# The second mixture-of-experts layer computed in units of 640 slots instead of tiles of 128

## The reference

```python
cap = int(1.25 * N / E)                       # 640
probs = softmax(x @ gate_w.T)
top2_w, top2_idx = top_k(probs, 2)
counts = bincount(a_e, length=E)
keep = counts <= cap                          # an expert with more tokens than that gives nothing
buf = zeros((E, cap + 1, H)).at[a_e, p].set(x[tok_id])
h = silu(einsum('ech,efh->ecf', buf, w1) + b1[:, None, :])
y = einsum('ecf,egf->ecg', h, w2) + b2[:, None, :]
contrib = y[a_e, p] * (a_w * valid)[:, None]
out = contrib.reshape(N, 2, H).sum(axis=1)
```

## Time and profile before

| | us |
|---|---|
| median of three runs | 2154.68 |
| the profiled execution | 2156.69 |
| its span, first to last instruction | 2154.9 |
| first gather of the second experts starts | 1972.19 |
| last scatter of the second experts starts | 2112.67 |
| the sums are read back, first DMA issued | 2119.80 |
| PE, DVE, ACT, POOL busy over the whole span | 1854.9, 1239.3, 914.2, 438.1 |

### The profile page before, as it was taken

One profiled execution on the slowest core, in us unless ns is written; L12 is line 12 of the kernel. 1 busy time (PEld: TensorE's weight loads), 2 busy tenths in 40 slices (PEclk: granted clock), 3 DMA queues, 4 the chain that ended last, 5 costly groups with the idle time before them and its releaser, 6 DMA issues. The chain is left out here.

```text
span 2154.9 us, 35159 instructions
## 1 busy us (share of the span) xinstructions
PE 1854.9 (86%) x9600; PEld 1119.4 (52%) x9601; DVE 1239.3 (58%) x2822; ACT 914.2 (42%) x1337; POOL 438.1 (20%) x573
## 2 busy tenths in 40 slices
PE   7899999999999999996599999999994885068771
PEld 4423333333333333363388888888884565037550
DVE  4588888888888888744711111111113796946335
ACT  3336666666666667753022233223331520031330
POOL 2210000000000000030023333333331001202771
PEclk9979999999999999998799999999997998586995
DMA  4511111111111111054433433443442001141224
GB/s 148 182 45 31 30 37 30 30 36 31 30 34 33 30 33 33 16 164 142 159 90 110 111 99 104 115 114 108 97 111 80 1 1 63 63 153 27 46 38 156
DMA packets 103317, 159.34 MB, mean 74 GB/s; under 512 B 20704, under 2 KB 79392, under 8 KB 97760
## 3 DMA queue, kind: packets, MB, share of 16 engines
q1 hardware_dynamic: 69712, 118.46, 16.9%
q0 software_dynamic: 22656, 24.51, 6.5%
q10 hardware_dynamic: 10896, 15.73, 2.1%
HBM read 124.19 MB, written 49.02 MB: 80 GB/s over the span
## 5 line engine op out<-in xcount | busy, mean ns | idle before, releaser
L552 DVE TENSOR_REDUCE unit_max<-ps_ring 128x1 f32<-128x512 f32 x1024 | 655.4, 686 | 83.7 <-PE ps_ring L429 73.4
L538 ACT ACTIVATE w<-ps_scores 128x1024 f32<-128x1024 f32 x512 | 510.0, 1023 | 266.2 <-PE ps_scores L504 254.4
L429 PE MATMUL ps_ring<-k_stack,q_stack 96*128 96x512 bf16 x1024 | 371.7, 391 | 9.8 <-POOL v_padded L392 9.2
L504 PE MATMUL ps_scores<-q_stack,k_stack 98*128 98x512 bf16 x1024 | 305.7, 380 | 0.1
L1495 PE MATMUL m_ps_h<-m_xt,m_w 128*128 128x256 f32 x1248 | 278.0, 381 | 0.8 <-DVE m_xt L1546 0.8
L1507 PE MATMUL m_ps_y<-w,m_ht 128*128 x1248 | 275.8, 379 | 0.0
L451 PE MATMUL ps_o<-w,v_padded 128*32 128x512 f32 x2048 | 272.8, 605 | 0.6 <-ACT w L538 0.6
L429 PEld LDWEIGHTS ps_ring<-k_stack,q_stack 96*128 96x128 bf16 x1024 | 102.1, 100 | 317.3 <-DVE unit_max L552 232.2
L1495 PEld LDWEIGHTS m_ps_h<-m_xt,m_w 128*128 128x128 f32 x1248 | 238.6, 191 | 34.0 <-DVE m_xt L1546 1.2
L1507 PEld LDWEIGHTS m_ps_y<-w,m_ht 128*128 128x128 f32 x1248 | 234.2, 190 | 30.3
L1527 ACT ACTIVATE m_ht<-m_ps_h,m_w 128x256 f32<-128x256 f32 x312 | 131.0, 471 | 143.7 <-PE m_ps_h L1495 143.7
(11 more groups left out here) (230 smaller groups left out, 2008.9 us busy)
## 6 DMA issues: line engine op xcount, KB each, us to landing
m_w<-in_w SPq DMA_DIRECT2D x39, 1028.0 KB
rows<-g_rows SPq DMA_DIRECT2D x16, 512.0 KB, 2.9
y<-sums SPq DMA_DIRECT2D x16, 512.0 KB, 7.1
q_parts<-qk_part SPq DMA_DIRECT2D x16, 384.0 KB, 3.6
k_parts<-qk_part SPq DMA_DIRECT2D x16, 384.0 KB, 3.8
q_stack<-q_parts SPq DMA_DIRECT2D x64, 96.0 KB
k_stack<-k_parts SPq DMA_DIRECT2D x64, 96.0 KB
xt<-in_xt ACTq DMA_DIRECT2D x8, 512.0 KB, 4.2
```

Source lines behind the costliest of these rows:

```text
L429: nc.tensor.matmul(out[:, :], qs[0:STACK, u, qt * P:(qt + 1) * P], ks[0:STACK, u, half * HALF:(half + 1) * HALF], start=True, stop=True).t ...
L504: mm = nc.tensor.matmul(p_s[kt % 2][:, half * HALF:(half + 1) * HALF], ks[:, u, kt * P:(kt + 1) * P], qs[:, u, half * HALF:(half + 1) * HALF],
L538: nc.scalar.activation(pt[:, kt, :], p_s[kt % 2][:, :], ACT.Exp, scale=SCALE)\
L552: nc.vector.tensor_reduce(unit_max[:, u % 2, half, qt:qt + 1], src[:, :], axis=AX.X, op=ALU.max).then_inc(ring_used, 1)
```

## The change

The stage is written anew as `stage_experts_columns`. Its unit is an expert: 640 slots.

- The five gathers of an expert are issued together, those of expert e+1 before the scatters of expert e, and each has an index tile of its own. They signal per PSUM bank: chunks 0 and 1, chunks 2 and 3, chunk 4.
- The weights stand and the tokens stream, 320 at a time (two halves of an expert). The first product thus has its features on the partitions, and the turn back and its copy are gone. The bias is a per-partition operand of ScalarE's SiLU, which reads PSUM itself; VectorE's bias addition is gone. The bias is loaded as 128 x 16 values and no longer as 128 x 2048.
- VectorE copies the turned tokens out of PSUM instead of ScalarE, 512 columns at a time.
- The second product is unchanged per 128 tokens, but has two PSUM tiles in turn. `m_y` holds a whole expert, twice.
- The five scatters of an expert follow each other without a wait between them. Before the first one GpSimd waits for those of the expert before.
- `indices(e)` copies ten index columns for an expert at once. It waits until all scatters of expert e-2 have landed, and it stands on VectorE behind the second biases of expert e-2.
- The stage is written out for all 8 experts, without a loop, and without the separate semaphore instructions.

```diff
-def stage_experts(nc, c, tiles, fixed, F, w1, w2, b1, b2, func, rows, sums):
...
+def stage_experts_columns(nc, c, per, w1, w2, b1, b2, func, rows, sums, finish=None):
+    FC, T = D // P, per * P
+    TH = T // 2
+    BANKS = (per + 1) // 2
+    with ExitStack() as stack:
+        mem = Mem(nc, stack)
+        ig = [mem.sb(f"m_ig{j}", [P, 1], I32) for j in range(2 * per)]
+        isc = [mem.sb(f"m_is{j}", [P, 1], I32) for j in range(2 * per)]
+        xg = [mem.sb(f"m_x{u}", [P, per, D]) for u in range(2)]
+        xt = [mem.sb(f"m_xt{u}", [P, KC, T]) for u in range(2)]
+        ht = [mem.sb(f"m_ht{u}", [P, FC, T]) for u in range(2)]
+        ys = [mem.sb(f"m_y{u}", [P, per, D]) for u in range(2)]
+        p_x = [mem.ps(f"m_ps_x{n}") for n in range(BANKS)]
+        p_h = [mem.ps(f"m_ps_h{f}") for f in range(FC)]
+        p_y = [mem.ps(f"m_ps_y{n}") for n in range(2)]
+        idx_g, idx_s = mem.sem("m_idx_g"), mem.sem("m_idx_s")
+        gathered = [[mem.sem(f"m_gathered{u}{n}") for n in range(BANKS)] for u in range(2)]
+        added = mem.sem("m_added")
+        x_turned, x_copied = mem.sem("m_x_turned"), mem.sem("m_x_copied")
+        h_made, act_done = mem.sem("m_h_made"), mem.sem("m_act_done")
+        y_made, y_biased, y_scaled = mem.sem("m_y_made"), mem.sem("m_y_biased"), mem.sem("m_y_scaled")
+        def chunks(n):
+            return range(2 * n, min(2 * n + 2, per))
+        def bank_of(half):
+            return (0, 1) if half == 0 else (2,)
+        with nc.Block() as block:
+            @block.gpsimd
+            def _(pool):
+                def gather(e):
+                    for j in range(per):
+                        pool.wait_ge(idx_g, e * per + j + 1)
+                        pool.indirect_dma_start(out=xg[e % 2][:, j, :], out_offset=None, in_=rows,
+                                                in_offset=bass.IndirectOffsetOnAxis(ap=ig[e % 2 * per + j][:, :], axis=0))\
+                            .then_inc(gathered[e % 2][j // 2], 16)
+                def add(e):
+                    wait_from(pool, added, e * per * 16)
+                    for j in range(per):
+                        pool.wait_ge(idx_s, e * per + j + 1)
+                        pool.wait_ge(y_scaled, e * per + j + 1)
+                        pool.indirect_dma_start(out=sums,
+                                                out_offset=bass.IndirectOffsetOnAxis(ap=isc[e % 2 * per + j][:, :], axis=0),
+                                                in_=ys[e % 2][:, j, :], in_offset=None, bounds_check=N - 1,
+                                                oob_is_err=False, compute_op=ALU.add).then_inc(added, 16)
+                gather(0)
+                for e in range(E):
+                    if e + 1 < E:
+                        gather(e + 1)
+                    add(e)
+                if finish is None:
+                    pool.wait_ge(added, E * per * 16)
 ...
+            @block.tensor
+            def _(pe):
+                def turn_x(e, n):
+                    pe.wait_ge(gathered[e % 2][n], (e // 2 + 1) * len(chunks(n)) * 16)
+                    wait_from(pe, x_copied, (e - 1) * BANKS + n + 1)
+                    for k in range(KC):
+                        for j in chunks(n):
+                            at = (k * 2 + j % 2) * P
+                            mm = nc.tensor.transpose(p_x[n][:, at:at + P], xg[e % 2][:, j, k * P:(k + 1) * P],
+                                                     c.ident[:, :])
+                    mm.then_inc(x_turned, 1)
+                def first_product(e, half):
+                    pe.wait_ge(x_copied, e * BANKS + bank_of(half)[-1] + 1)
+                    for f in range(FC):
+                        wait_from(pe, act_done, (2 * e + half - 1) * FC + f + 1)
+                        for k in range(KC):
+                            mm = nc.tensor.matmul(p_h[f][:, 0:TH], w1[:, e * KC + k, f * P:(f + 1) * P],
+                                                  xt[e % 2][:, k, half * TH:(half + 1) * TH],
+                                                  start=(k == 0), stop=(k == KC - 1))
+                        mm.then_inc(h_made, 1)
+                def second_product(e, j):
+                    pe.wait_ge(act_done, (2 * e + ((j + 1) * P > TH)) * FC + FC)
+                    wait_from(pe, y_biased, e * per + j - 1)
+                    for f in range(FC):
+                        mm = nc.tensor.matmul(p_y[(e * per + j) % 2][:, 0:D], ht[e % 2][:, f, j * P:(j + 1) * P],
+                                              w2[:, e * FC + f, :], start=(f == 0), stop=(f == FC - 1))
+                    mm.then_inc(y_made, 1)
+                for n in range(BANKS):
+                    turn_x(0, n)
+                for e in range(E):
+                    first_product(e, 0)
+                    first_product(e, 1)
+                    for j in range(per):
+                        second_product(e, j)
+                        if j >= per - BANKS and e + 1 < E:
+                            turn_x(e + 1, j - (per - BANKS))
+            @block.scalar
+            def _(act):
+                def middle(e, half):
+                    for f in range(FC):
+                        act.wait_ge(h_made, (2 * e + half) * FC + f + 1)
+                        nc.scalar.activation(ht[e % 2][:, f, half * TH:(half + 1) * TH], p_h[f][:, 0:TH], func,
+                                             bias=b1[:, e * FC + f:e * FC + f + 1]).then_inc(act_done, 1)
+                def scale(e, j):
+                    t = e * per + j
+                    act.wait_ge(y_biased, t + 1)
+                    nc.scalar.activation(ys[e % 2][:, j, :], ys[e % 2][:, j, :], ACT.Copy,
+                                         scale=c.gains[:, t:t + 1]).then_inc(y_scaled, 1)
+                for e in range(E):
+                    middle(e, 0)
+                    middle(e, 1)
+                    for j in range(per):
+                        scale(e, j)
 ...
+            @block.vector
+            def _(dve):
+                def indices(e):
+                    wait_from(dve, added, (e - 1) * per * 16)
+                    for j in range(per):
+                        nc.vector.tensor_copy(ig[e % 2 * per + j][:, :], c.gather[:, e * per + j:e * per + j + 1])\
+                            .then_inc(idx_g, 1)
+                    for j in range(per):
+                        nc.vector.tensor_copy(isc[e % 2 * per + j][:, :], c.scatter[:, e * per + j:e * per + j + 1])\
+                            .then_inc(idx_s, 1)
+                def copy_x(e, n):
+                    dve.wait_ge(x_turned, e * BANKS + n + 1)
+                    cols = len(chunks(n)) * P
+                    nc.vector.tensor_copy(xt[e % 2][:, :, n * 2 * P:n * 2 * P + cols],
+                                          p_x[n][:, :].rearrange("p (c n) -> p c n", c=KC)[:, :, 0:cols])\
+                        .then_inc(x_copied, 1)
+                def bias_y(e, j):
+                    t = e * per + j
+                    dve.wait_ge(y_made, t + 1)
+                    nc.vector.tensor_tensor(ys[e % 2][:, j, :], p_y[t % 2][:, 0:D], b2[:, e, :], ALU.add)\
+                        .then_inc(y_biased, 1)
+                indices(0)
+                indices(1)
+                for n in range(BANKS):
+                    copy_x(0, n)
+                for e in range(E):
+                    for j in range(per):
+                        bias_y(e, j)
+                        if j >= per - BANKS and e + 1 < E:
+                            copy_x(e + 1, j - (per - BANKS))
+                    if e + 2 < E:
+                        indices(e + 2)
+        mem.clear()
...
-            b1 = m.sb("b1_1", [P, E, D])
+            b1 = m.sb("b1_1", [P, E * KC])
...
-                act.dma_start(b1[:, :, :], a.b1_1.partition_broadcast(P)).then_inc(loaded, 16)
+                act.dma_start(b1[:, :], a.b1_1).then_inc(loaded, 16)
...
-            stage_experts(nc, c, CAP * E, CAP, D, w1, w2, b1, b2, ACT.Silu, rows[1], sums[1])
+            stage_experts_columns(nc, c, CAP, w1, w2, b1, b2, ACT.Silu, rows[1], sums[1])
```

More of the change, by code:

```diff
@@ L1166, in stage_experts @@
         y_made, y_biased, y_scaled = mem.sem("m_y_made"), mem.sem("m_y_biased"), mem.sem("m_y_scaled")
-        spare_p = mem.sem("m_spare")
-        halves = F // HW
+        def chunks(n):
+            return range(2 * n, min(2 * n + 2, per))
+        def bank_of(half):
+            return (0, 1) if half == 0 else (2,)
         with nc.Block() as block:
-            def steps(eng, body):
-                peeled_ends(eng, tiles // STEP, body)
             @block.gpsimd
             def _(pool):
[L1176 to L1205, removed]
-                        elif u - 1 in (0, fixed):
-                            wait_apart(pool, spare_p, added[0], before[0])
-                            wait_apart(pool, spare_p, added[1], before[1])
-                        add(t + u - 1, (u - 1) % 2)
-                steps(pool, body)
```

(39 more changed lines are left out.)

117 lines of the change are left out of this document (7 added, 110 removed).

## The result

The kernel after takes 2159.44 us, median of 17 runs (2155.43 to 2167.17), against 2154.96 for the kernel before (2152.97 to 2158.85, 17 runs): ratio 1.0023, 95% interval [1.0013, 1.0032]. A second set gave 1.0024 [1.0012, 1.0036]. The forecast was 2158.3 with 2149 to 2166 and "the same", up to 2159.0, as the likeliest. By the two intervals the change costs 3 to 8 us; whether that is more than the 0.2% that the prediction drew as its line isn't decided.

A forecast was written before the change was run, and what follows sets the result against it. GpSimd's preparation of 80 transfers was taken as the bound. The stage: 17.3 + 12.45 + 89.0 + 13.9 + 3.9 + 7.5 = 144.05 us against 140.48; thus 2154.68 + 3.6 = 2158.3 us, range 2149 to 2166.

The forecast's parts named there:

- the 3.6 us that the stage was to lose: Second experts' stage, first gather to last scatter's start: 144.05 us forecast against 140.48 before.
- GpSimd's preparation is the bound, and stays: Second experts: GpSimd's serial preparation of 40 gathers and 40 scatters sets the pace before and after; chance 0.74.
- The 0.30 us stays: GpSimd's gap before each transfer remains without separate semaphore instructions; rival: the gathers' gap goes, 12 us faster, chance 0.12.
- The beginning, 17.3 us: Stage's start: first scatter 17.3 us after the first gather, between 16.4 (full clock) and 18.4 (half clock until 1985.4).
- The border: Between experts GpSimd waits 2.9 us for the landing and 1.0 to the gather: cycle 17.8 us instead of 16.66.
- the rival of the shorter border: Between experts GpSimd answers in 0.5 us: 3.5 us less, 2155; its chance is included in the 0.74.
- The last border, 3.9 us: From expert 6's fifth scatter to expert 7's first: 3.9 us, waiting for the landing.
- The stage, +3.6 us: Second experts, first gather to last scatter's start: 144.05 us against 140.48, 3.6 us more.
- The landings: Rival at seven borders: five scatters in flight land slower, 3.95 us for an empty one; 7 us more, 2165; chance 0.05.
- What stands behind is the same.: Everything after the stage's last scatter takes the same time, so only the stage's 3.6 us is added.
- TensorE at half clock: Rival in the expert cycles: TensorE at half clock becomes the bound, 20.8 us against 17.8; 2169 to 2179; chance 0.07.
- The rule on descriptors: Rival: descriptor generation is small, scatters overlap, TensorE sets the pace at full clock; 50 us less, 2105; chance 0.02.

The follow-up runs named there:

- 80 more turns: The kernel before with the ten transposes of each expert's middle layer done twice: 2155.27 us, ratio 1.0001.
- 448 unused bytes: The kernel after with 448 unused bytes per partition behind the second experts' biases, so the store's tiles start at a multiple of 512: 2157.47 us, ratio 1.0005.
- indices early: The kernel after with gather index copies ahead of the second biases, without a wait: 2149.36 us; with own scatter index tiles too: 2148.97 us.
- TensorE kept busy: The kernel after with 15 extra fp32 products per expert (1 to 6) into an unread PSUM bank: 2157.55 us, ratio 1.0011 to before.
- gathers two ahead: The kernel with all indices early, plus a third gather buffer and an index tile per gather, gathers running two experts ahead: 2148.81 us, ratio 0.9966 to before.
- the gathers-two-ahead one with the tiles moved: The kernel with gathers two experts ahead, plus 448 unused bytes that put the store's tiles at a multiple of 512: 2144.89 us, ratio 0.9949 to before.

## Why the prediction was right

The time lies in the range, and the mechanism in the stage is the one forecast: GpSimd runs dry at each border, because the gather indices wait for the scatters. That the number came so close (2158.3 against 2159.4) is luck: of the 3.6 us that the stage was to lose, the profiles show 0.7 on average, and the rest of the 4.5 us lies where nothing was forecast.

- *GpSimd's preparation is the bound, and stays.* Right: 101.4 us for 80 instructions, cycles free of other idle once the wait is gone, 80 more turns at no cost.
- *The 0.30 us stays.* Right: it stands between instructions with no wait of their own (0.30 <-issue). That rival fell.
- *The beginning, 17.3 us.* 16.7, 18.2 and 18.4 in the three profiles of after (the third with 448 unused bytes); the bounds were 16.4 and 18.4. The 16 records of the first products took 5.29, 6.73 and 6.75 us, at a granted clock up to the first scatter of 0.69, 0.63 and 0.63.
- *The border.* Forecast 2.9 to the landing and 1.0 to the answer, cycle 17.8; measured 17.08. Three profiles have 1.62 us of idle there where 2.3 were forecast. The mis-sized term is the answer: the gather starts 0.43 us after the copy (2005.11 to 2005.54, 2040.88 to 2041.31); the landing took 2.74. The 1.0 had been read from the stage's first gather, where it is 0.72 in after as well (1976.42 to 1977.14), and from a scatter behind ScalarE, and neither is a gather at a border. Five cycles: 85.4 us instead of 89.0. This is the rival of the shorter border, an answer in 0.5 us for 3.5 us less and 2155: it came true. At the first border, behind expert 0, 4.95 were forecast from the last scatter's start to the gather, and 4.17, 3.82 and 4.15 measured. The 0.42 us that an expert loses against 16.66 make 2.1 over five.
- *The last border, 3.9 us.* 3.93 in two profiles, 6.60 in the first, where TensorE came late: its granted clock was 0.65 in the 13.9 us before, and 1.00 in the same stretch of the second profile.
- *The stage, +3.6 us.* Measured 140.1, 140.7 and 143.3 against 140.5 and 140.8: -0.6 to +2.8, by the means +0.7. The form of the forecast holds; its size was too large. In the second profile the 3.9 us under the forecast 144.05 are 3.6 in the five cycles and 1.1 at the first border, less 0.9 at the beginning.
- *The landings.* Five in flight did not slow them: 2.74 us at four of the six borders of the first profile, 3.74 behind expert 0, 4.36 once. That rival fell.
- *Smaller loads, 0.* Right: VectorE waits 9.60 and 9.68 us for `gamma` in the two profiles of after, 9.43 and 9.59 before.
- *"What stands behind is the same."* This step failed. The store at the end takes 1.45 us longer, from the smaller bias tile, which the prediction had costed as a load only. Another 0.26 us lies between the last scatter and the loads that follow it (7.39 against 7.13), in the profiles of after and of the kernels with indices early or TensorE kept busy; with the gathers two ahead it is 8.0. Nothing tells its cause.
- *TensorE at half clock.* The clock fell as that rival had it, to 0.81 in the stage, but TensorE didn't become the bound of the cycles: with the clock restored they were no shorter, and the time 1 to 2 us less. A price shows only at the ends of the stage, up to 1.5 us in the first products and 2.7 at the last border of one profile. The Trainium skill, "TensorE: Matmul & The Clock Gate", section "HAM oscillation — how this bites in real kernels", warns of this pattern; the trace agrees on the clock (0.81), and not on a price in each turn: cycles of 17.08 us at a clock of 1.00 (from 2075.43) and of 0.70 (from 2058.35) are alike.
- *The rule on descriptors.* The Trainium skill, "DMA: Bandwidth & Descriptors", section "Anatomy of one DMA — SWDGE (gpsimd) path", calls their generation small beside completion. With scatters in flight together completion did vanish from all but the borders, and GpSimd still needed 1.55 + 0.30 us for each; of the 1.55, 1.27 don't depend on the rows. Here the measurement decides against the rule, and the 2105 us that it gave are far off.

What stays open: the stage's mean difference (0.7 us), the store (1.45) and the 0.26 make 2.4 of the 4.5 us between the medians (3.9 in the second set). With the tiles moved after lost 3.9 us in ratio and the gathers-two-ahead kernel 3.7 where the store explains 1.45; the intervals, some 2.5 us to each side, don't tell the rest from nothing. The moved bytes shift the gather and result tiles too; no gain shows in the stage, but no run moved these alone.

The best kernel run is the gathers-two-ahead one with the tiles moved, 2144.89 us, 0.5% below the kernel before.

## What to carry to other kernels

A copy of an index is a cheap instruction in a dear place: ask of each wait which later instructions stand behind it on its engine. Here the five gather copies needed no wait at all; put ahead of the biases, they were worth the whole loss and 5 us more. Where an engine's preparation of transfers is the bound, look at fewer transfers and at its dry stretches; 80 transposes more on another engine changed nothing here. A tile that changes its size moves all that are allocated behind it: compare the untouched stages too.

## What the runs showed of the hardware

- Stores of 512 KB from tiles that start 64 bytes over a multiple of 512 in a partition landed in a median of 3.9 us (3.0 to 4.7), from a multiple of 512 in 3.1 (2.8 to 3.3); for eight in a row that is 1.45 us.
- An accumulating indirect scatter of 1 KB rows costs GpSimd 1.41 us for 64 rows and 1.55 for 128, and 0.30 us pass to the next transfer, with separate semaphore instructions between them (before) and without (after).
- Later gathers landed later than the first ones: the turns of expert 2 started 4.1 and 5.1 us after their last gather's start (2006.87 to 2010.96, 2009.41 to 2014.50), against 2.8 in the same kernel at the stage's start (1978.47 to 1981.24). Scatters in flight aren't needed for it: the first five gathers of the stage landed in a median of 2.8 us, the next five, with no scatter issued yet, in 4.5, and those of expert 2, all behind the last scatter's landing, in 4.6. What makes the difference no run shows.
